# A DLRM interaction tower: the tenth lookup table of odd tiles gathered instead of looked up

## The reference

```python
all_vecs = jnp.concatenate([dense_proj[:, None, :], sparse_embs], axis=1)
interactions = jnp.einsum('bnd,bmd->bnm', all_vecs, all_vecs)
interact_flat = interactions[:, rows, cols]
h = jnp.concatenate([z, r_dense_proj], axis=1)
h = jnp.maximum(h @ W_top1 + b_top1, 0.0)
h = jnp.maximum(h @ W_top2 + b_top2, 0.0)
y = h @ W_top3
```

## Time and profile before

| what | value |
|---|---|
| median of 3 runs | 369.66 us (369.25 to 370.26) |
| profiled execution | 369.59 us |
| its span, first to last instruction | 367.8 us |
| TensorE / GpSimd / VectorE / ScalarE busy | 334.5 / 244.4 / 243.9 / 138.6 us |
| mean granted TensorE clock | 0.995 of full speed |

### The profile page before, as it was taken

The page is one execution under the profiler, slowest core; times in us unless marked ns, Lnnn a source line. Parts: engine busy times, 40 slices in busy tenths (PEclk is TensorE's granted clock), DMA queues, the critical chain, the costliest instruction groups (busy, mean ns, idle before and its releaser), DMA issues.

```text
span 367.8 us, 14433 instructions
## 1 busy us (share of the span) xinstructions
PE 334.5 (91%) x6192; PEld 309.7 (84%) x6192; DVE 243.9 (66%) x702; ACT 138.6 (38%) x232; POOL 244.4 (66%) x260
## 2 busy tenths in 40 slices
PE   0775689999899899999999999999999999999986
PEld 0765689999799898989899898989899898998865
DVE  4999998989456684669567694659656694702210
ACT  2246332536043260435324260435414270437122
POOL 5877777777777777777777777777777777720000
PEclk9999999999899999999999999999999999999999
DMA  6999943231243211531134111531235111310000
GB/s 191 285 256 252 287 133 125 61 124 53 60 148 126 58 53 50 163 115 50 54 106 167 57 51 50 157 121 50 57 81 190 50 55 52 78 29 2 20 2 0
DMA packets 16758, 36.94 MB, mean 100 GB/s; under 512 B 5661, under 2 KB 8733, under 8 KB 16735
## 3 DMA queue, kind: packets, MB, share of 16 engines
q1 hardware_dynamic: 8479, 19.80, 17.6%
q0 software_dynamic: 8192, 16.79, 16.7%
q10 hardware_dynamic: 64, 0.01, 0.0%
HBM read 36.57 MB, written 0.01 MB: 99 GB/s over the span
## 4 chain that ended last, share of the span: by engine, by line
PE 84%; DVE 6%; DMA 3%; issue 3%; SPq 2%; ACT 1%; DVEq 0%
PE gram L418 14%; PE hid L384 13%; PE look_odd L338 8%; PE look_odd L340 8%; PE look_ps L338 7%; PE look_ps L340 7%; PE vec_act L311 7%; PE hid L392 7%; DVE onehot L572 4%; PE hid L338 4%; PE hid L340 4%; DMA raw<-tbl 3%; DVE look_lo L580 2%; PE small L353 1%; SPq L245 1%
## 5 line engine op out<-in xcount | busy, mean ns | idle before, releaser
L292 POOL DMA_INDIRECT vecs<-tbl,ids_sb x256 | 244.2, 954 | 80.5 <-issue 77.4
L572 DVE TENSOR_SCALAR onehot<-step_ids,row_no 125x256 fp32r<-125x256 int32 x640 | 201.6, 386 | 45.0 <-PE look_odd L340 26.3
L338 PE MATMUL look_odd<-onehot,look_hi 125*128 125x256 f32 x256 | 69.7, 307 | 6.3 <-DVE look_lo L580 6.2
L547 ACT COPY vecs_T<-vec_act 128x512 f32<-128x512 f32 x64 | 45.8, 729 | 76.1 <-PE vec_act L311 75.3
L338 PE MATMUL look_ps<-onehot,look_hi 125*128 125x256 f32 x256 | 66.4, 296 | 4.2 <-DVE look_lo L580 2.1
L340 PE MATMUL look_odd<-onehot,look_lo 125*128 125x256 f32 x256 | 64.0, 284 | 0.0
L340 PE MATMUL look_ps<-onehot,look_lo 125*128 125x256 f32 x256 | 62.9, 282 | 0.0
L418 PE MATMUL gram<-vecs_T 128*27 128x26 f32 x4096 | 52.8, 193 | 8.9 <-issue 4.6
L418 PEld LDWEIGHTS gram<-vecs_T 128*27 128x27 f32 x4096 | 43.9, 104 | 17.9 <-issue 14.5
L338 PEld LDWEIGHTS look_odd<-onehot,look_hi 125*128 125x128 f32 x256 | 49.2, 192 | 8.2 <-DVE look_lo L580 7.0
L338 PEld LDWEIGHTS look_ps<-onehot,look_hi 125*128 125x128 f32 x256 | 48.8, 191 | 5.2 <-DVE look_lo L580 5.0
(11 more groups left out here) (70 smaller groups left out, 277.7 us busy)
## 6 DMA issues: line engine op xcount, KB each, us to landing
step_ids<-look_ids SPq DMA_DIRECT2D x15, 640.0 KB
raw<-tbl SPq DMA_DIRECT2D x10, 448.0 KB
vecs<-tbl,ids_sb POOLq DMA_INDIRECT x256
dense_new<-dense SPq DMA_DIRECT2D x8, 128.0 KB
dense_T<-dense SPq DMA_DIRECT2D x8, 128.0 KB, 2.4
raw<-tbl SPq DMA_DIRECT2D x10, 52.0 KB
step_ids<-look_ids SPq DMA_DIRECT2D x1, 512.0 KB
w_sb<-w SPq DMA_DIRECT2D x1, 512.0 KB
```

The lines of the kernel that those rows point to most:

```text
L292: nc.gpsimd.indirect_dma_start(out=vecs[j][:, k, :], out_offset=None, in_=tables[k], in_offset=bass.IndirectOffsetOnAxis(ap=ids_sb[:, t, k ...
L338: nc.tensor.matmul(bank, look_hi[:, f, ch, :], onehot[:, i % SLOTS, c, :], start=ch == 0, stop=False)
L547: return engine_copy(vecs_T[j][:, :, lo:lo + GROUP], bank[:, :, :].rearrange("d v b -> d b v"))
L572: last = nc.vector.tensor_scalar(onehot[:, i % SLOTS, c, :], step_ids[a][0:LOOK_K, f - a * LOOKUPS // 2, :], row_no[0:LOOK_K, ch:ch + 1], ...
```

## The change

From pair 2 on, that is for all lookups done in the loop, the last small table (table 9 of ten) is no longer looked up. GpSimd gathers its rows for both tiles of a pair into `last_rows`, two indirect DMAs behind the even tile's sixteen, by a 17th column of ids. TensorE leaves out units 8 and 9 of odd tiles and instead turns the two tiles of rows into the half of the bank where that table's columns went, at the end of the odd tile; VectorE makes no one-hots for these units, and the counts of the left-out units are added to unit 7's. In even tiles pairs_out moves from ahead of unit 2 to behind it. ScalarE's relu2 goes ahead of its unit 7. SP loads four tables' ids instead of five for odd steps from pair 2 on. In the unrolled end TensorE's and ScalarE's orders change: turns of tile 15 come later, layer2's second half ahead of the last gram half.

```diff
@@ -70,6 +70,8 @@
...
+ROWS_FROM = 2
+
 PARTS = 4
@@ -107,7 +109,8 @@
...
-        ids_sb = sb("ids_sb", [P, tiles, GATHERS], I32)
+        ids_sb = sb("ids_sb", [P, tiles, GATHERS + 1], I32)
+        last_rows = sb("last_rows", [P, 2, D])
         vecs = [sb(f"vecs{j}", [P, ROWS, D]) for j in range(2)]
@@ -172,7 +175,8 @@
...
         gathered = [[sem(f"gathered{j}_{h}") for h in range(2)] for j in range(2)]
-        first_ids_in = sem("first_ids_in")
+        first_ids_in, last_rows_in = sem("first_ids_in"), sem("last_rows_in")
+        last_turned = sem("last_turned")
         step_ids_in = [sem(f"step_ids_in{a}") for a in range(2)]
@@ -276,7 +280,7 @@
...
                     load_step(2 * r, 0, r)
-                    load_step(2 * r + 1, 1, r)
+                    load_step(2 * r + 1, 1, r, slice(0, STEP_IDS - 1))
                     load_dense(r - 1)
@@ -294,11 +298,23 @@
...
+                def gather_last(pair):
+
+                    if pair > ROWS_FROM:
+                        pool.wait_ge(last_turned, pair - ROWS_FROM)
+                    for j in range(2):
+                        nc.gpsimd.indirect_dma_start(
+                            out=last_rows[:, j, :], out_offset=None, in_=look_tables[LOOKUPS - 1],
+                            in_offset=bass.IndirectOffsetOnAxis(ap=ids_sb[:, 2 * pair + j, GATHERS:GATHERS + 1], axis=0),
+                        ).then_inc(last_rows_in, 16)
+
                 pool.wait_ge(tile_ids_in, 16)
...
                     gather(t)
+                    if t % 2 == 0 and t // 2 >= ROWS_FROM:
+                        gather_last(t // 2)
@@ -321,7 +337,7 @@
...
-                def look_up(s, a, pair, i):
+                def look_up(s, a, pair, i, used=1):
@@ -339,7 +355,15 @@
...
                                                 start=False, stop=ch == LOOK_CH - 1)
-                    last.then_inc(onehot_used, 1)
+                    last.then_inc(onehot_used, used)
+
+                def turn_last(pair):
+
+                    pe.wait_ge(last_rows_in, 2 * 16 * (pair - ROWS_FROM + 1))
+                    for j in range(2):
+                        lo = PAIR + j * P
+                        last = nc.tensor.transpose(look_ps[DUO_BANK[DUOS - 1]][:, lo:lo + P], last_rows[:, j, :], ident[:, :])
+                    last.then_inc(last_turned, 1)
@@ -448,7 +472,7 @@
...
                     def unit(i):
-                        look_up(t + 2, j, pair + 1, i)
+                        look_up(t + 2, j, pair + 1, i, 3 if mlp and j == 1 and i == LOOKUPS - 3 else 1)
@@ -457,9 +481,11 @@
...
                     turn_group(n, k, 1)
-                    if not first:
+                    if not first and not (mlp and j == 0):
                         pairs_out(t - 1, j, pair)
                     unit(2)
+                    if mlp and j == 0:
+                        pairs_out(t - 1, j, pair)
                     unit(3)
@@ -469,6 +495,15 @@
...
                     turn_group(n, k, 2)
+                    if mlp and j == 1:
+                        unit(6)
+                        turn_group(n, k, 3)
+                        unit(7)
+                        gram_first(t, j, pair)
+                        gram_second(j)
+                        layer3(pair - 1)
+                        turn_last(pair + 1)
+                        return
                     unit(6)
@@ -478,8 +513,6 @@
...
                         gram_second(j)
-                    if mlp and j == 1:
-                        layer3(pair - 1)
                     unit(9)
@@ -503,18 +536,18 @@
...
                 last = tiles - 1
-                turn_half(last, 1, pairs - 1, 0)
                 gram_first(last - 1, 0, pairs - 1)
                 pairs_out(last - 2, 0, pairs - 1)
-                turn_half(last, 1, pairs - 1, 1)
                 layer1(pairs - 2, 0, look=False)
...
                 layer1(pairs - 2, 1)
+                turn_half(last, 1, pairs - 1, 0)
+                layer2(pairs - 2, 0)
+                pairs_out(last - 1, 1, pairs - 1, bank=pairs_end)
+                turn_half(last, 1, pairs - 1, 1)
                 gram_first(last, 1, pairs - 1)
-                pairs_out(last - 1, 1, pairs - 1, bank=pairs_end)
-                layer2(pairs - 2, 0)
+                layer2(pairs - 2, 1)
                 gram_second(1)
-                layer2(pairs - 2, 1)
                 pe.wait_ge(dense_in, 16 * pairs)
@@ -563,7 +596,7 @@
...
-                def make_unit(s, a, i, f, half):
+                def make_unit(s, a, i, f, half, count=1):
@@ -572,7 +605,7 @@
...
                             row_no[0:LOOK_K, ch:ch + 1], None, ALU.is_equal)
-                    last.then_inc(onehot_made, 1)
+                    last.then_inc(onehot_made, count)
@@ -580,14 +613,16 @@
...
-                def tile(t, j, pair, first=False, look=True):
+                def tile(t, j, pair, first=False, look=True, rows=False):
                     made = units(j)
+
+                    full = LOOKUPS - 2 if rows else LOOKUPS
...
                         if look:
-                            make_unit(t + 2, j, *made[i])
+                            make_unit(t + 2, j, *made[i], 1 + LOOKUPS - full if i == full - 1 else 1)
@@ -596,7 +631,7 @@
...
                         turn(t - 1)
-                    for i in range(TURN_UNIT, LOOKUPS):
+                    for i in range(TURN_UNIT, full):
                         unit(i)
@@ -621,7 +656,7 @@
...
                     tile(2 * r, 0, r)
-                    tile(2 * r + 1, 1, r)
+                    tile(2 * r + 1, 1, r, rows=True)
                 last = tiles - 1
@@ -681,7 +716,10 @@
...
                     tables = bank.rearrange("d (v j b) -> d v j b", v=2, j=2)
-                    act.wait_ge(onehot_used, LOOKUPS * s + i + 1)
+                    if f == LOOKUPS - 1 and not isinstance(pair, int):
+                        act.wait_ge(last_turned, pair - ROWS_FROM + 1)
+                    else:
+                        act.wait_ge(onehot_used, LOOKUPS * s + i + 1)
                     if isinstance(pair, int) and pair == 0:
@@ -731,11 +769,11 @@
...
                         merge(1, pair, False)
+                    if mlp and j == 1:
+                        relu2(pair - 1)
                     unit(7)
...
                         relu1(pair - 1, 0)
-                    if mlp and j == 1:
-                        relu2(pair - 1)
                     unit(9)
@@ -771,17 +809,17 @@
...
                 last = tiles - 1
-                for q in range(HALF_GROUPS):
-                    copy(last, 1, q)
                 copy_pairs(last - 2, 1)
-                for q in range(HALF_GROUPS, GROUPS):
-                    copy(last, 1, q)
                 merge(1, pairs - 1, True)
...
                 relu1(pairs - 2, 1)
+                for q in range(HALF_GROUPS):
+                    copy(last, 1, q)
                 copy_pairs(last - 1, 0, pairs_end)
+                for q in range(HALF_GROUPS, GROUPS):
+                    copy(last, 1, q)
                 relu2(pairs - 2)
@@ -810,7 +848,7 @@
...
         "dense": dense,
-        "ids": np.ascontiguousarray(ids[:, large].reshape(-1, P, GATHERS).transpose(1, 0, 2)),
+        "ids": np.ascontiguousarray(ids[:, large + small[-1:]].reshape(-1, P, GATHERS + 1).transpose(1, 0, 2)),
         "look_ids": np.ascontiguousarray(ids[:, small].T.reshape(2, LOOKUPS // 2, -1, 2 * P).transpose(0, 2, 1, 3)
```

## The result

The changed kernel is slower: 374.61 us median of 4 runs (373.25 to 375.12) against 369.46 for the kernel before (368.27 to 370.26), a ratio of 1.0131, with a 95% interval from 1.0089 to 1.0173. The direction was the forecast's, the size was not: 371.9 us was predicted, and the time lies above the range. The profiled execution of the changed kernel took 374.99 us, with a span of 373.2, so 1.8 us lie around it as before.

A forecast was written before the change was run, and what follows sets the result against it. TensorE was taken to bound the kernel, with GpSimd only 1.9 us a pair faster. Terms summing to +1.05 us, plus 1.2 for the clock, turned the profiled 369.59 into 371.8, forecast as 371.9; range 369.2 to 373.8.

The forecast's parts named there:

- GpSimd becomes the bound: In the loop, GpSimd's gathers take 42.6 us a pair against TensorE's 40.2; TensorE waits 2.4 us every pass.
- The pin: Loop's last pass: the turn of tile 13's second half waits for gathered rows, starting at 298.0, only 1.1 us earlier.
- Tile 13 and the loop's end: After that turn: two units fewer, -1.7 us; gram slowed by gathers, +1.2; loop ends at 330.9.
- gram_first(14): Unrolled end, tile 14's first gram half: bare wait for ScalarE about 1.25 us, +0.8; its second half of gathers, +0.1.
- The bare waits: Unrolled end: TensorE waits uncovered for ScalarE's copies, 1.15 us before layer1 (+0.8) and 1.2 before gram_first of tile 15 (+1.2).
- layer2 ahead of the last gram: Unrolled end: layer2's second half moves earlier, +1.7 us; pairs_out about 2.4 after the last gram matmul, -1.5; net +0.2.
- The issue gap: A 0.94 us gap without releaser before the very last gram matmul may shift; half taken off, -0.45 us.
- The clock: One fall of TensorE's granted clock to half speed on the path after 298.0, +1.2 us.

The follow-up runs named there:

- e4: The changed kernel with only pair 2's tenth-table rows gathered, and those rows turned again in later pairs; 365.59 us, ratio 0.9838 to the kernel before.
- e5: The changed kernel without tile 15's sixteen gathers, old rows being turned instead; 371.57 us, ratio 1.0013 to the kernel before.
- e3: The kernel before the change with twelve more gathers that nobody reads; 377.93 us, ratio 1.0179.
- e11: The changed kernel with layer3's sixteen small matmuls done twice in the loop, 32 more TensorE instructions; 373.16 us, ratio 1.0060 to the kernel before.
- e7: The kernel before the change with an unrolled end reordered to put turns and layers behind the waits; 375.81 us, ratio 1.0108.

## Why the prediction was wrong in size

By its steps, with the change's profile beside each:

- *GpSimd becomes the bound*: right. The turns at 214.80 and 299.92 are two pairs apart, 42.6 us each, as worked out, and GpSimd never waits for TensorE. TensorE waits for rows at these two turns, 1.90 and 1.74 us, and not at tile 11's between them, where the fall of the clock at 216 had used the slack up; predicted were 2.4 us in every pass. The saved time is gone by tile 13: e4, without eight of the ten gathers ahead, turns there at 293.34.
- *The pin*: **the first step that failed**, 298.0 predicted, 299.92 measured, +1.9. The 16th gather started at 297.38 and not 296.0: GpSimd started 0.1 later, the three long gathers at the start took 5.11 together against 4.36 in the kernel before, a fourth took 1.22, and the ten `last_rows` gathers ahead 0.97 each instead of 0.95. Then landing took 2.42 us and 0.12 to the turn, 2.54 instead of 2.0: I had read it from when the queue emptied in the earlier trace rows, not from a wait. Here too the packets of this gather end at about 299.25, 0.55 us before its rows count as landed at 299.80. In the six profiles with all of the added gathers ahead of tile 13 the pin lies between 299.2 and 300.3, so most of this is the kernel's and some tenths are one execution's. The forecast had the turn only 1.1 us earlier than before (0.9 by the timeline's 298.92); an error of 1.9 made it 1.0 later.
- *Tile 13 and the loop's end*: 32.9 us from the turn predicted, 33.3 measured, +0.4. The gram took 3.74 where 3.5 was assumed: the 3.48 of the earlier trace rows is among the shortest, and the kernel before's others in the loop take up to 4.08. Another 0.16 is the reading of 299.08 for 298.92.
- *gram_first(14)*: its start was right (1.25 us of wait predicted, 1.3 measured), but it lay wholly under the gathers and took 2.6 us to pairs_out where I had 1.5: +1.1. The slow pitch in the loop was known from the earlier trace rows; I spread its cost as a bound of 0 to 1.7 over tile 13 and "part of tile 14's", and put 0.1 where e5 shows 1.2 (0.45 to 1.2 over the builds).
- *The bare waits* of layer1 and of gram_first(15): right, 1.16 us (1.15 predicted) and 1.1 (1.2). layer2 ahead of the last gram: right, once the gap is taken off, 2.5 us to pairs_out (2.4).
- *The issue gap*: **wrong in sign**. I took half of 0.94 off; the end has 0.37 + 0.91 = 1.28 us, +0.8 over the 0.5 that I had left. The gaps' places, 254 to 256 counted instructions apart, fit the blocks of 256 in the rule of the Trainium skill ("Runtime: NRT & Kernel Launch", Instruction fetch mechanics). The traces disagree with its word that the crossing from one block to the next is mostly hidden: in and just behind stretches of narrow matmuls they show gaps of 0.2 to 2.5 us. That the engine waits for a fetch in them is an inference from the places; no trace row shows the fetch itself.
- *The clock*: the 1.2 us did not occur. It fell where the loop absorbs it.

The terms that failed make 1.9 + 0.4 + 1.1 + 0.8 = 4.2 us; the clock takes 1.2 off; that leaves 3.0 of the 3.15 us by which the span (373.2 against 370.05) exceeds the forecast's. Of the 4.2 us, 1.3 (0.2 of tile 13's gram and gram_first(14)'s 1.1) come of one fact that I had priced in the loop and not followed into the end: the gathers now run beside everything up to 340 us. The terms are those of one execution of each kernel; over executions and builds the pin alone moved by 1.0 us.

## What to carry to other kernels

When work is moved to an engine whose queue has no gaps, its price is its whole pitch (instruction and issue gap together), and what it may cost for nothing is the difference of the two engines' periods, here 1.9 us a pair against 2.5 us of added gathers; the busy share tells neither. Past that margin, what the other engine saves is worth nothing. Ask also what then runs beside the tail: the gathers did not only pin the loop, they slowed the narrow matmuls that follow it. And in straight code of many tiny instructions, taking waits out may only make room for gaps; weave the narrow work between wide work and look at the next trace.

## What was unexpected of the hardware

- 256 gram matmuls take 2.33 us with GpSimd idle (e5) and 3.48 to 4.06 with gathers beside them (the changed kernel's 3.74, e3's 3.93, e4's 4.06), though the two share no semaphore in that stretch. Matmuls 256 columns wide keep their 0.12 us pitch under the same gathers (starts at 328.31, 328.43 and 328.55 in the changed kernel).
- TensorE's gaps without a releaser in the end stand at places 127 or 128 matmuls with their loads apart, or a multiple, stay there over builds and move with the code (e11), but their size goes from 0.2 to 2.5 us. In the changed kernel, e5 and e7 TensorE resumes from two neighbouring gaps 3.6 to 3.8 us apart (355.42 and 359.25; 352.83 and 356.41; 354.53 and 358.26). The kernel before and e3 have a single gap in this stretch, of 0.94 and 1.76 us, so it is not shown that a fixed time for each stretch of code sets the size; it stays open.
- The same early gathers took from 0.94 to 1.96 us in different builds while the tables were loading. The last of all 268 gathers starts between 337.31 (e3) and 340.07 us (e11); among the builds on the changed loop the spread is 0.7 us.
